# A router product of 16 rows, with the halves added on VectorE

## The chip, the cores and the metric

The kernel runs on one core of a Trainium2 chip. The metric is the device time of one execution in microseconds (us), as the median of several runs. TensorE (PE) does the matmuls and the transposes, VectorE (DVE) and ScalarE (ACT) the elementwise work and what is taken out of TensorE's banks, GpSimd (POOL) some preparation and the indirect transfers, SyncE (SP) issues the other transfers.

## The reference, cut to what matters

An attention layer (gated, in groups of 64 tokens, with a linear part over the whole sequence) is followed by a residual and a layer norm, a mixture of experts on its output, another residual and norm. The router chooses two of eight experts for each token, from eight logits a token:

```
x = _layernorm(x + attention(x, ...))       # 8 blocks of 512 tokens, 256 wide
shared = new_gelu(xf @ Wfc_s + bfc_s) @ Wproj_s + bproj_s
logits = xf @ Wr                            # Wr: 256 x 8
probs = jax.nn.softmax(logits, axis=-1)
topk_p, topk_i = jax.lax.top_k(probs, 2)
...                                         # gates from topk_p, eight experts, summed
x = _layernorm(x + shared + routed)
```

A wrong choice of an expert would be a large error, so the logits have to be as exact as the other products.

## The kernel before, in words

TensorE's products use a rounded format (`F32R`). To come near full precision each operand is split: a high part (the rounded value) and a low part (the value less its high part). A product is then three matmuls, high by low, low by high and high by high, which add up in one bank (`three`, lines 675 to 679).

The program has two parts with a barrier between them. The first, `attention`, goes over the eight blocks of 512 tokens in steps b = 0 to 10. Step b does the attention of block b, the output product and second norm of block b - 1, and transposes, splits and routes block b - 2. Steps 3 to 6 are a loop at run time (`Fori`), the others are written out. From step 8 on, the shared expert's first products are laid beside the rest. The second part, `experts`, begins with the softmax over all logits and does everything else.

Each engine has a list of its own, written by hand, and does it in order. What ties the lists together are semaphores: an instruction counts one up when it is done, another waits for a number. A wait holds all that stands behind it on the same engine. There is no planner: the order in the source is the order on the engine.

The path of the logits for block c = b - 2:

- At the end of step b TensorE multiplies the router's weights with the transposed x1 (line 844). The result, 8 experts by 512 tokens, stands in rows 0 to 7 of bank 7. The count is `lt_mm`.
- ScalarE, after the last rounding of `u`, copies it to `lgT` (line 488, recorded as line 378, `lt_ev`). `lgT` has 128 rows, of which the others are zero.
- In step b + 1 TensorE, after the value products, transposes `lgT` in four tiles of 128 tokens into bank 7 (lines 746 to 750, `lg_mm`).
- ScalarE, after the last value block, copies the 8 columns of each tile to `logits` (line 440, recorded as line 378, `lg_ev`), and goes on with the normalised x1 and the next block's xn (`normed`, line 396).
- TensorE meanwhile is in the output product (lines 755 to 765). Its four token tiles go to the halves of banks 6 and 7. The third (t = 2) writes bank 7, so it waits for `lg_ev` (line 758). After it come the keys and scores, the gate products, the key-value product, the transposes and the product of `u`.

VectorE in a step: statistics and reciprocal roots for two norms (`stats`, `rstd`), the rotary embedding and the heads (lines 562 to 571), the residual's addition (line 575), statistics of the output product straight from its banks (line 576), the norm (581, 585), the attention scores, the low parts. The list of a step then begins anew. A `link` makes VectorE wait for its own operation, where the next reads what it wrote.

Of the kernel before, what the change touches and what calls it, by code (L numbers as in the profile page):

```python
# [23 lines left out]
F32 = mybir.dt.float32  # L24
F32R = mybir.dt.float32r
# [3 lines left out]
ALU = mybir.AluOpType  # L29
# [3 lines left out]
P = 128  # L33
B, T, D = 8, 512, 256
# [6 lines left out]
NE = 8  # L41
KD = D // P
KE = E // P
KH = HID // P
TT = T // P
# [25 lines left out]
def is_int(n):  # L71
    return isinstance(n, int)
# [111 lines left out]
def attention(nc, a, shared):  # L184
    ident, ones2, logits = (shared[k] for k in ("ident", "ones2", "logits"))
# [5 lines left out]
    with ExitStack() as ctx:  # L191
# [11 lines left out]
                                                   ("wg", [P, KD, E]), ("wo", [P, KE, D])))  # L203
        wrh, wrl = pair("wr", [P, KD, NE])
        bv2 = sb("bv2", [P, E], F32R)
# [16 lines left out]
        z = sb("z", [P, TT, D])  # L222
        lgT = sb("lgT", [P, T])
        x1 = sb("x1", [P, TT, D])
        x1T = sb("x1T", [P, KD, T])
# [151 lines left out]
        def _(act):  # L377
# [35 lines left out]
            def step(b):  # L413
# [22 lines left out]
                if at(B + 2):  # L436
                    beside(7)
                if not is_int(b) or b >= 3:
                    act.wait_ge(lg_mm, b - 2)
                    copy(logits[:, bass.ds((b - 3) * TT, TT), :], bank[7][:, :].rearrange("p (t n) -> p t n", t=TT)[:, :, 0:NE]).then_inc(lg_ev, 1)  # L440
                if last:
# [44 lines left out]
                if last:  # L486
                    act.wait_ge(lt_mm, c + 1)
                    copy(lgT[0:NE, :], bank[7][0:NE, :]).then_inc(lt_ev, 1)
                if at(B):
# [12 lines left out]
        def _(dve):  # L502
# [32 lines left out]
            def beside(*chunks):  # L535

                for j in chunks:
                    dve.wait_ge(hh_rd, j + 1)
                    tt(e_hl[j % 4], e_h[j % 2], e_hh[j % 4].bitcast(F32), ALU.subtract).then_inc(hl_rd, 1)

            def step(b):
                main, ahead, o, last = stages(b)
# [18 lines left out]
                if main:  # L561
                    for s in range(2):
                        dve.wait_ge(q_ev, 4 * b + 2 * s + 2)
                        last_i = tt(qkr[:, s, :], qk[:, s, :], rope[:, s, :], ALU.mult)
                        last_i.then_inc(qkr_rd, 1)
                    dve.wait_ge(qkr_rd, 2 * b + 1)
                    stt(heads[:, 0, :], qkr[:, 0, :], vec[:, GQ:GQ + 1], offs[:, 0, :], ALU.mult, ALU.add)
                    link(stt(heads[:, 1, :], qkr[:, 0, :], vec[:, GK:GK + 1], offs[:, 1, :], ALU.mult, ALU.add))
                    dve.wait_ge(qkr_rd, 2 * b + 2)
                    stt(heads[:, 1, :], qkr[:, 1, :], vec[:, GK + 1:GK + 2], heads[:, 1, :], ALU.mult, ALU.add).then_inc(heads_rd, 1)  # L570
                    stt(heads[:, 0, :], qkr[:, 1, :], vec[:, GQ + 1:GQ + 2], heads[:, 0, :], ALU.mult, ALU.add).then_inc(heads_rd, 1)
                if o:
                    yo = [bank[6 + t // 2][:, t % 2 * D:t % 2 * D + D] for t in range(TT)]
# [84 lines left out]
            bias_rows(bpj[SHW][0:BR, :], bpj_raw[SHW][:, :])  # L658
            link(nc.vector.tensor_copy(wrh[:, :, :], wr[:, :, :]))
            tt(wrl[:, :, :], wr[:, :, :], wrh[:, :, :].bitcast(F32), ALU.subtract).then_inc(tab_rd, 1)  # L660
            step(1)
# [5 lines left out]
            link.end(B - 4)  # L667
            for b in range(B - 1, B + 2):
                step(b)

        @block.tensor
        def _(pe):
# [46 lines left out]
            def step(b):  # L719
# [113 lines left out]
                if last:  # L833
# [9 lines left out]
                    for k in range(KD):  # L843
                        last_i = three(bank[7][0:NE, :], wrh[:, k, :], wrl[:, k, :], x1h[:, k, :], x1l[:, k, :], k == 0, k == KD - 1)
                    last_i.then_inc(lt_mm, 1)
# [12 lines left out]

STEP_LINKS, BLOCK_LINKS, SMALL_LINKS = 33, 10, 6

# [756 lines left out]
```

## Time and profile before

| | us |
|---|---|
| median of 3 runs | 1000.14 |
| lowest, highest | 999.05, 1000.84 |
| the profiled execution | 1000.27 |
| its span, first to last instruction | 998.4 |
| TensorE busy | 936.1 (94%) |
| VectorE busy | 752.9 (75%) |
| ScalarE busy | 566.6 (57%) |
| attention part | to about 337 of the span |

TensorE's matmuls are pipelined: one starts before the one ahead has ended, so the distance of two starts is what a matmul costs, and its duration in a row is longer. A square bracket at the end of a row of the order of time says how long the engine was idle before it, and what ended that.

### The profile page before, as it was taken

To read this page: it belongs to the slowest core of one execution; us is meant where nothing else is said; L and a number is where in the kernel's file an instruction comes from. 1 tells how busy PE (TensorE), PEld (TensorE's weight loads), DVE (VectorE), ACT (ScalarE), POOL (GpSimd) and SP (SyncE) were. 2 spreads that over 40 slices of the span, in tenths; PEclk is the share of its full clock that TensorE was granted. 3 is DMA by queue.
4 is the path that set the end of the run, shared out by engine and by line. 5 is a ranking of instruction groups with operands and counts; after the bars stand their busy time and mean duration, and the time that the engine had idled before them with its cause. 6 is when DMAs were issued, how large, how long until landed. Compare 5 with 4: busy or idle time off the path is not lost.

```text
span 998.4 us, 17975 instructions
## 1 busy us (share of the span) xinstructions
PE 936.1 (94%) x5998; PEld 830.3 (83%) x5998; DVE 752.9 (75%) x1823; ACT 566.6 (57%) x1008; POOL 234.3 (23%) x170
## 2 busy tenths in 40 slices
PE   4979999999997988899999999999999989999995
PEld 3767788788876777799999999999999989999994
DVE  5799889888876589677777777777777879984846
ACT  5625556655645532355555555555555768874654
POOL 0050000000000000324444444444444444421000
PEclk9979999999999998999999999999999999999998
DMA  4130323231333422245555555555555678877302
GB/s 155 58 117 30 129 69 126 68 127 52 106 114 126 145 44 85 72 130 127 133 138 132 141 155 147 132 134 135 136 143 143 177 194 226 237 223 222 106 22 85
DMA packets 66869, 125.88 MB, mean 126 GB/s; under 512 B 13629, under 2 KB 52384, under 8 KB 60289
## 3 DMA queue, kind: packets, MB, share of 16 engines
q1 hardware_dynamic: 48144, 101.02, 30.4%
q0 software_dynamic: 14976, 20.54, 12.4%
q10 hardware_dynamic: 3696, 3.67, 1.1%
q8 instruction: 28, 0.46, 0.2%
q14 instruction: 25, 0.20, 0.1%
HBM read 92.40 MB, written 31.75 MB: 124 GB/s over the span
## 4 chain that ended last, share of the span: by engine, by line
PE 57%; DVE 6%; ACT 1%; DMA 1%; issue 1%; POOL 0%; DVEq 0%
PE bank L1460 28%; PE bank L1503 27%; PE bank L1488 2%; DVE s_hl L1382 1%; DVE s_acc L1256 1%; DMA s_xb<-x_rows,s_token 1%; DVE s_until_map L1258 1%; DVE s_until_map L1257 1%; DVE s_acc L1344 0%; POOL residual_sums L1080 0%; ACT s_hh L1130 0%; PE bank L1457 0%; ACT s_h L1126 0%; DVE s_until_map L1259 0%; PE bank L1523 0%
## 5 line engine op out<-in xcount | busy, mean ns | idle before, releaser
L1126 ACT ACTIVATE s_h<-bank,k_bfc 128x512 f32<-128x512 f32 (+1 forms) x248 | 154.6, 623 | 248.0 <-PE bank L1503 236.2
L1382 DVE TENSOR_TENSOR s_hl<-s_h,s_hh 128x512 fp32r<-128x512 f32 (+1 forms) x248 | 151.8, 613 | 144.0 <-ACT s_hh L1130 142.9
L1080 POOL DMA_INDIRECT residual_sums<-s_y,s_dest x78 | 132.8, 1703 | 233.0 <-DVE s_y L1330 216.6
L1071 POOL DMA_INDIRECT s_xb<-x_rows,s_token x78 | 84.8, 1087 | 382.3 <-DVE s_dest L1272 342.3
L1130 ACT ACTIVATE s_hh<-s_h 128x512 fp32r<-128x512 f32 (+1 forms) x248 | 141.4, 570 | 11.4 <-ACT s_h L1126 1.4
L1503 PE MATMUL bank<-k_uh,k_wfc1h 128*128 128x512 f32 (+1 forms) x448 | 139.6, 361 | 0.5 <-PEq L191 0.5
L1460 PE MATMUL bank<-s_wpj0l,s_hh 128*128 128x256 f32 x448 | 126.0, 281 | 1.4 <-DVE s_hl L1382 1.4
L1460 PE MATMUL bank<-s_wpj0h,s_hh 128*128 128x256 f32 x448 | 126.0, 281 | 0.0
L1460 PE MATMUL bank<-s_wpj0h,s_hl 128*128 128x256 f32 x448 | 125.8, 281 | 0.0
L1460 PE MATMUL bank<-k_wpj1l,s_hh 128*128 128x256 f32 x400 | 113.2, 283 | 0.2 <-DVE s_hl L1382 0.2
L1460 PE MATMUL bank<-k_wpj1h,s_hh 128*128 128x256 f32 x400 | 113.1, 283 | 0.0
L1460 PE MATMUL bank<-k_wpj1h,s_hl 128*128 128x256 f32 x400 | 113.0, 283 | 0.0
L1503 PEld LDWEIGHTS bank<-k_uh,k_wfc1h 128*128 128x128 f32 x448 | 82.5, 190 | 10.4 <-issue 0.6
L1460 PEld LDWEIGHTS bank<-s_wpj0l,s_hh 128*128 128x128 f32 x448 | 84.5, 189 | 5.5 <-DVE s_hl L1382 1.6
L1460 PEld LDWEIGHTS bank<-s_wpj0h,s_hl 128*128 128x128 f32 x448 | 85.5, 191 | 3.4
L1460 PEld LDWEIGHTS bank<-s_wpj0h,s_hh 128*128 128x128 f32 x448 | 84.4, 188 | 0.0
L1503 PE MATMUL bank<-k_xTl,s_wfc0h 128*128 128x512 f32 (+1 forms) x224 | 83.7, 374 | 0.6 <-issue 0.6
L1503 PE MATMUL bank<-k_xTh,s_wfc0l 128*128 128x512 f32 (+1 forms) x224 | 81.3, 363 | 0.0
L1503 PE MATMUL bank<-k_xTh,s_wfc0h 128*128 128x512 f32 (+1 forms) x224 | 80.8, 361 | 0.0
L1503 PE MATMUL bank<-k_uh,k_wfc1l 128*128 128x512 f32 (+1 forms) x224 | 79.8, 356 | 0.0
L1460 PEld LDWEIGHTS bank<-k_wpj1l,s_hh 128*128 128x128 f32 x400 | 75.8, 189 | 3.9 <-DVE s_hl L1382 0.6
L1460 PEld LDWEIGHTS bank<-k_wpj1h,s_hl 128*128 128x128 f32 x400 | 75.6, 189 | 3.3
(297 smaller groups left out, 2159.2 us busy)
## 6 DMA issues: line engine op xcount, KB each, us to landing
k_wstage<-wall SPq DMA_DIRECT2D x50, 1024.0 KB, 5.6
s_x_in<-x SPq DMA_DIRECT2D x8, 512.0 KB, 4.2
s_x_res<-x SPq DMA_DIRECT2D x8, 512.0 KB, 4.7
x_rows<-s_x SPq DMA_DIRECT2D x8, 512.0 KB, 3.5
residual_sums<-s_x SPq DMA_DIRECT2D x8, 512.0 KB, 4.2
x_parts<-s_x1h SPq DMA_DIRECT2D x8, 512.0 KB, 2.6
x_parts<-s_x1l SPq DMA_DIRECT2D x8, 512.0 KB, 3.7
k_uh<-x_parts SPq DMA_DIRECT2D x8, 512.0 KB, 4.9
```

The lines of the kernel that those rows point to most:

```text
L1071: pool.indirect_dma_start(xb[i][:, t, :], None, X1D, bass.IndirectOffsetOnAxis(token[:, at:at + 1].bitcast(U32), 0), bounds_check=N - 1).t ...
L1080: pool.indirect_dma_start(RES, bass.IndirectOffsetOnAxis(dest[:, at:at + 1].bitcast(U32), 0), y[:, t, :], None, bounds_check=N + S - 1, co ...
L1126: nc.scalar.activation(h[j % 2][:, cols], b[:, cols], ACT.Gelu_apprx_tanh, bias=bfc[w][:, j:j + 1]).then_inc(h_ev, 1)
L1130: nc.scalar.activation(hh[j % RING][:, cols], h[j % 2][:, cols], ACT.Copy).then_inc(hh_rd, 1)
L1256: tt(pick[:, at, :], row_of(IOTA, P), each(flat(slot_p[:, :, :]), P), ALU.is_equal)
L1257: link(tt(row, row_of(IOTA + P, COLS), each(flat(slot_c[:, :, :]), COLS), ALU.is_equal))
L1258: link(tt(signed, row, each(cst[:, CODE:CODE + 2 * NT][:, at], COLS), ALU.mult))
L1382: tt(hl[j % RING][:, cols], h[j % 2][:, cols], hh[j % RING][:, cols].bitcast(F32), ALU.subtract).then_inc(hl_rd, 1)
L1460: last = mm(o, hs[p][:, cols], wpj[w][ws][:, j, :], start=r is not None and j == 0 and p == 0 and t % 2 == 0, stop=j == KH - 1 and p == 2, ...
L1488: last = nc.tensor.transpose(b[:, t * P:(t + 1) * P], xb[1 - i][:, t, j * P:(j + 1) * P], ident[:, :])
L1503: last = mm(b[:, cols], wfc[w][ws][:, c, rows_], xs[i][:, c, cols], start=c == 0 and p == 0, stop=c == KD - 1 and p == 2)
```

## The change

The router's high and low weights stand side by side in one tile `wr_parts` of 16 columns. For each of the two halves of the contraction the product is now two matmuls: all 16 columns with the high part of x1 (high by high in rows 0 to 7, low by high in rows 8 to 15), and the 8 high columns with its low part, added to rows 0 to 7. The copy to `lgT` and the transposes carry 16 rows. The two halves are added after the transposes: `router_logits` on VectorE copies the lower half out of the bank to `lg_lo`, and adds it to the upper half into `logits`. ScalarE's copy at that place is gone. `router_logits` stands in VectorE's list between the heads and the residual's addition, and VectorE has a step more at the end.

```diff
-        wrh, wrl = pair("wr", [P, KD, NE])
+        wr_parts = sb("wr_parts", [P, KD, 2 * NE], F32R)
+        lg_lo = sb("lg_lo", [P, TT, NE])
@@ ScalarE, step
-                if not is_int(b) or b >= 3:
-                    act.wait_ge(lg_mm, b - 2)
-                    copy(logits[:, bass.ds((b - 3) * TT, TT), :], bank[7][:, :].rearrange("p (t n) -> p t n", t=TT)[:, :, 0:NE]).then_inc(lg_ev, 1)
...
-                    copy(lgT[0:NE, :], bank[7][0:NE, :]).then_inc(lt_ev, 1)
+                    copy(lgT[0:2 * NE, :], bank[7][0:2 * NE, :]).then_inc(lt_ev, 1)
@@ VectorE
+            def router_logits(c):
+
+                dve.wait_ge(lg_mm, c + 1)
+                by_tile = bank[7][:, :].rearrange("p (t n) -> p t n", t=TT)
+                link(nc.vector.tensor_copy(lg_lo[:, :, :], by_tile[:, :, NE:2 * NE]))
+                tt(logits[:, bass.ds(c * TT, TT), :], by_tile[:, :, 0:NE], lg_lo[:, :, :], ALU.add).then_inc(lg_ev, 1)
...
                     stt(heads[:, 0, :], qkr[:, 1, :], vec[:, GQ + 1:GQ + 2], heads[:, 0, :], ALU.mult, ALU.add).then_inc(heads_rd, 1)
+                if not is_int(b) or b >= 3:
+                    router_logits(b - 3)
                 if o:
...
-            link(nc.vector.tensor_copy(wrh[:, :, :], wr[:, :, :]))
-            tt(wrl[:, :, :], wr[:, :, :], wrh[:, :, :].bitcast(F32), ALU.subtract).then_inc(tab_rd, 1)
+            link(nc.vector.tensor_copy(wr_parts[:, :, 0:NE], wr[:, :, :]))
+            tt(wr_parts[:, :, NE:], wr[:, :, :], wr_parts[:, :, 0:NE].bitcast(F32), ALU.subtract).then_inc(tab_rd, 1)
...
-            for b in range(B - 1, B + 2):
+            for b in range(B - 1, B + 3):
                 step(b)
@@ TensorE, step
                     for k in range(KD):
-                        last_i = three(bank[7][0:NE, :], wrh[:, k, :], wrl[:, k, :], x1h[:, k, :], x1l[:, k, :], k == 0, k == KD - 1)
+                        mm(bank[7][0:2 * NE, :], wr_parts[:, k, :], x1h[:, k, :], start=k == 0, stop=False)
+                        last_i = mm(bank[7][0:NE, :], wr_parts[:, k, 0:NE], x1l[:, k, :], start=False, stop=k == KD - 1)
```

On VectorE, in the loop (steps 3 to 6), this is what stands from the last two operations of the heads on, before the change:

```order
L570 SCALAR_TENSOR_TENSOR s_heads<-s_qkr,s_vec,s_heads 128x512 [waits qk_roped]
L571 SCALAR_TENSOR_TENSOR s_heads<-s_qkr,s_vec,s_heads 128x512
L574 REGISTER_ALU
L575 TENSOR_TENSOR s_x_res<-s_x_res,s_ln 128x1024 [waits residual_loaded]
L576 ISA
L519 BN_STATS s_st<-bank 128x6 [waits o_product]
```

And after it, where the heads' lines are 575 and 576 and the residual's addition is line 582:

```order
L575 SCALAR_TENSOR_TENSOR s_heads<-s_qkr,s_vec,s_heads 128x512 [waits qk_roped]
L576 SCALAR_TENSOR_TENSOR s_heads<-s_qkr,s_vec,s_heads 128x512
L541 REGISTER_ALU
L543 COPY s_lg_lo<-bank 128x32 [waits logits_transposed]
L102 REGISTER_ALU
L544 ISA [waits vector_own]
L544 TENSOR_TENSOR k_logits<-bank,s_lg_lo 128x32
L581 REGISTER_ALU
L582 TENSOR_TENSOR s_x_res<-s_x_res,s_ln 128x1024 [waits residual_loaded]
L583 ISA
L517 BN_STATS s_st<-bank 128x6 [waits o_product]
```

The copy and the addition have come between the heads and the residual's addition, with the wait for the copy between them.

On ScalarE in the same steps, from the last value block on, before:

```order
L435 ACTIVATE s_v<-bank 128x512 [waits v_product]
L439 REGISTER_ALU
L378 ISA [waits logits_transposed]
L378 ACTIVATE k_logits<-bank 128x32
L442 REGISTER_ALU
L90 REGISTER_ALU [waits scales_ready]
L396 ACTIVATE s_x<-s_z,s_shift,s_rs 128x256 [waits x1_stored]
```

And after:

```order
L436 ACTIVATE s_v<-bank 128x512 [waits v_product]
L440 REGISTER_ALU
L90 ISA [waits scales_ready]
L397 ACTIVATE s_x<-s_z,s_shift,s_rs 128x256 [waits x1_stored]
```

ScalarE no longer waits for the transposes; the normalised x1 follows the value blocks directly. On TensorE the third tile of the output product keeps its wait (`logits_ready`), which is now counted by VectorE's addition.

## Rows read from the trace of the kernel before

**Rows 1.** Busy time by stretch: engines, clock, DMA share, GB/s

```profile
120.00:280.00 160.00, 160.00 (x919) 131.22 (x918) 134.89 (x395) 97.20 (x170) 0.00 (x0) 1.00 0.28 92
280.00:337.00 57.00, 49.08 (x301) 41.26 (x300) 32.75 (x105) 27.79 (x49) 0.00 (x0) 0.94 0.42 141
```

**Rows 2.** Order of time (start, duration, engine, line, operation), TensorE, end of step 2

```profile
120.29 0.40 PE L679 MATMUL bank<-s_x1h,s_wrh 128*8 128x512 f32 x1
...
121.21 0.39 PE L677 MATMUL bank<-k_xTl,s_wqkh 128*128 128x512 f32 x1
```

**Rows 3.** Order of time, step 3: third output tile and VectorE

```profile
132.67 0.28 PE L761 MATMUL bank<-s_bo,k_ones 128*128 128x256 f32 x1
...
133.35 1.22 DVE L575 TENSOR_TENSOR s_x_res<-s_x_res,s_ln 128x1024 f32<-128x1024 f32 x1
...
135.95 0.76 DVE L519 BATCH_NORM_STATS2 s_st<-bank 128x6 f32<-128x256 f32 x2 [0.71 <-PE bank L679]
```

**Rows 4.** Order of time, VectorE, end of step 3

```profile
149.18 0.69 DVE L528 TENSOR_TENSOR k_xTl<-s_xT,k_xTh 128x512 fp32r<-128x512 f32 x1 [1.17 <-ACT k_xTh L378]
```

**Rows 5.** Order of time, the same two places in step 6

```profile
234.42 0.28 PE L761 MATMUL bank<-s_bo,k_ones 128*128 128x256 f32 x1
...
235.04 1.22 DVE L575 TENSOR_TENSOR s_x_res<-s_x_res,s_ln 128x1024 f32<-128x1024 f32 x1
```

**Rows 6.** VectorE: line 1189 by itself, then order of time at three places

```profile
L1189 DVE TENSOR_TENSOR s_gates<-s_cnt x2: 189/192/195, 351.2 to 351.3; 128x32 f32<-128x32 f32 x2
...
410.05 0.23 DVE L1267 COPY s_found<-bank 128x78 f32<-128x78 f32 x1
410.31 0.24 DVE L1268 SCALAR_TENSOR_TENSOR s_code<-s_found,bank 128x78 f32<-128x78 f32 x1
...
410.97 0.23 DVE L1271 TENSOR_TENSOR s_code<-s_empty,s_cst 128x78 f32<-128x78 f32 x1
...
164.99 0.74 DVE L568 SCALAR_TENSOR_TENSOR s_heads<-s_qkr,s_vec,s_offs 128x512 f32<-128x512 f32 x1
165.85 0.75 DVE L570 SCALAR_TENSOR_TENSOR s_heads<-s_qkr,s_vec,s_heads 128x512 f32<-128x512 f32 x1
```

**Rows 7.** Order of time: TensorE waits for VectorE at 341 us

```profile
341.07 0.69 DVE L1382 TENSOR_TENSOR s_hl<-s_h,s_hh 128x512 fp32r<-128x512 f32 x1 [1.29 <-ACT s_hh L1130]
...
341.81 0.39 PE L1457 MATMUL bank<-k_bpj,k_ones 128*128 128x256 f32 x1 [0.70 <-DVE s_hl L1382]
342.04 0.29 PE L1460 MATMUL bank<-k_wpj1l,s_hh 128*128 128x256 f32 x1
```

**Rows 8.** Order of time, the two places in step 7

```profile
267.11 1.22 DVE L575 TENSOR_TENSOR s_x_res<-s_x_res,s_ln 128x1024 f32<-128x1024 f32 x1
...
268.33 0.28 PE L761 MATMUL bank<-s_bo,k_ones 128*128 128x256 f32 x1
```

**Rows 9.** Order of time, step 8, TensorE and VectorE

```profile
291.50 0.66 PE L749 MATMUL bank<-k_ident,s_lgT 128*128 128x128 f32 x4 [0.68 <-ACT s_lgT L378]
...
295.07 0.28 PE L761 MATMUL bank<-s_bo,k_ones 128*128 128x256 f32 x1
...
296.10 0.16 DVE L523 SCALAR_TENSOR_TENSOR s_shift<-s_mean,s_rs 128x4 f32<-128x4 f32 x1
...
298.79 1.41 DVE L519 BATCH_NORM_STATS2 s_st<-bank 128x6 f32<-128x256 f32 x4
...
307.33 0.58 PE L707 MATMUL bank<-k_bpj,k_ones 128*128 128x256 f32 x1 [3.99 <-DVE s_wvh L539]
```

**Rows 10.** Order of time, step 9, ScalarE and TensorE

```profile
321.20 0.20 ACT L378 ACTIVATE k_logits<-bank 128x32 f32<-128x32 f32 x1 [0.49 <-PE bank L749]
...
323.40 1.22 PE L684 MATMUL bank<-k_ident,s_x 128*128 128x128 f32 x8 [2.25 <-ACT s_x L396]
```

**Rows 11.** Busy time by stretch, in steps 1 and 9

```profile
75.00:80.00 5.00, 3.74 (x10) 1.58 (x9) 4.77 (x14) 0.69 (x1) 0.00 (x0) 1.00 0.00 0
324.00:328.00 4.00, 4.00 (x18) 3.42 (x17) 1.29 (x2) 2.94 (x6) 0.00 (x0) 0.57 0.96 330
```

More of the change, by code:

```diff
@@ L855, in _ @@
             steps(pe, step, end=B + 3)
-STEP_LINKS, BLOCK_LINKS, SMALL_LINKS = 33, 10, 6
+STEP_LINKS, BLOCK_LINKS, SMALL_LINKS = 34, 10, 6
 def experts(nc, a, out, shared):
```

## The prediction

> **What bounds the kernel now.** I read the busy time by stretch first. In the attention part (up to 337 us) TensorE is busy without a break from 120 to 280 us, at full granted clock, while VectorE and ScalarE are not full; only in the last 57 us of that part has TensorE holes [rows 1]. So in the steps of the loop a microsecond taken from TensorE's order, or put into it, is a microsecond of the kernel, unless the part's own order of waits says otherwise. The rest of the kernel (661 us) is not touched, and starts behind a barrier that TensorE reaches last. All that matters lies in the steps b = 2 to 9 and the short step 10.
>
> The next view is the order of time in single steps, and there one distance decides. The output product of a step has four token tiles; the third writes bank 7, in which the router's transposed logits stand, so it waits on the count that says that the logits are taken out. In step 3 it starts at 132.67 us [rows 3]. VectorE at that time is still at the rotary heads, and starts the next thing, the residual's addition of line 575, only at 133.35. The same distance stands in all four steps that wait so (3 to 6): 0.68 us in the first, 0.62 in the last [rows 3, 5]. This order costs nothing today, because ScalarE takes the logits.
>
> **The change, part by part.**
>
> *The product.* Two products of 512 columns for each half of the contraction take the place of three. The router's products follow one another like the others: from the third at 120.29 to the first of the next group at 121.21 are four starts, 0.23 us each [rows 2], and that although each has only 8 rows of output. Sixteen rows instead of 8 should change nothing in that. Two products less are 0.46 us of TensorE in each of eight steps, 3.7 us in all, if each counts.
>
> *The logits move from ScalarE to VectorE*, and stand in VectorE's order behind the heads: a copy of the lower half out of the bank, a wait for the copy, an addition that releases TensorE. Nothing like them stands there in the trace, so I bound them. An operation on 128x32 takes 0.19 us [rows 6]. Behind a linked operation the next started 0.03 us after its end in straight code (410.05 + 0.23 to 410.31) and 0.12 us after it in the loop, where register instructions stand between (164.99 + 0.74 to 165.85) [rows 6]. From VectorE's end to TensorE's start are 0.05 us (341.07 + 0.69 to 341.81), and the product behind such a wait then needs 0.23 us until the next starts, where 0.12 is usual for 256 columns: 0.11 us to get going again [rows 7]. I take 0.19 + 0.12 + 0.19 + 0.05 = 0.55 us from the old start of line 575 to TensorE's start, and 0.11 for the restart. The low end is the straight-code gap and no restart, 0.46; the high end has 0.23 for each operation (the 78-wide ones), a gap of 0.12 ahead of the copy too, and the restart: 0.86.
>
> At 78 elements a copy out of a bank took 0.23 us and an addition out of SBUF (410.97) 0.23 us as well, so the bank is no dearer a source here [rows 6]. The Trainium skill (VectorE: DVE Perf Modes, the section on the errata of trn2) gives a source in PSUM 62 cycles more than one in SBUF, an estimate of 0.065 us each at its clock. By that rule the two operations would cost 0.13 us more in a step than the 0.19 of an operation out of SBUF, and the sum would be 0.5 us higher.
>
> *Steps 3 to 6: a new wait.* Does VectorE come earlier because TensorE does? No: its work in a step begins with line 528, for which it waits 1.17 us on ScalarE's rounding of the transposed input [rows 4], which hangs on TensorE's work of the step before, ahead of the router's product; from there to line 575 I see no idle time on it worth naming. So VectorE's time is fixed against TensorE's past, and TensorE, 0.46 us earlier, only waits longer. Its third tile starts at (line 575's old start) + 0.55: that is 0.65 (mean of 0.68 and 0.62) + 0.55 = 1.20 us later than today, plus 0.11. The 0.46 us saved are already swallowed in this. Four steps by 1.31 are **+5.2 us**, with 4 x (0.65 + 0.46) = 4.4 and 4 x (0.65 + 0.86) = 6.0 as ends. The idle time that TensorE shows is 1.20 + 0.46 = 1.7 us each time. What stands behind it in its order (second half of the output product, keys, gate) is as late. VectorE is not made later still: its addition and first statistics end about 0.5 us later, and it has to wait for the second half of the product anyway (0.71 us today [rows 3], about 1.4 then).
>
> *Step 7.* It is the last with attention, and has no statistics of a further input, so VectorE is early: line 575 starts at 267.11 and the third tile at 268.33 [rows 8]. The pair ends at about 267.6, TensorE comes at 267.9. No wait; the product of step 6 is worth its **-0.46**. With a pair of 0.86 us it would be 0.1 late, so this term is safe.
>
> *Step 8.* The saving of the product of step 7 is worth nothing: TensorE waits 0.68 us today for ScalarE's copy of it [rows 9], and ScalarE is held by VectorE there; if the copy did follow, it would be -0.46. The logits now come behind a whole normalisation on VectorE. Its last operation starts at 296.10; plus about 0.1 to the copy and 0.46 that is 296.7, where the third tile starts at 295.07 today [rows 9]. TensorE stops 1.6 us and ends the product at 295.07 + 1.6 + 0.1 + 26 x 0.12 = 299.9. Most is covered: VectorE reads the second half at 298.79 + 2 x 0.35 = 299.5 today [rows 9], and would then at 299.9 + 0.2 = 300.1 (the 0.2 as in step 3: 132.67 + 3.1 against 135.95 [rows 3]). VectorE's chain from there is what TensorE waits 3.99 us for at 307.33 [rows 9]. So **+0.54**, from 0.3 to 0.8. Its cover is the wait for the residual's transfer ahead of line 575; without it the pair would add its own 0.4.
>
> *Steps 8 and 9: the products*, in stretches where TensorE is busy up to the next wait: **-0.46** and **-0.46**.
>
> *Step 9, ScalarE.* Today it waits 0.49 us for TensorE's transposes and takes the logits in 0.20 us ahead of the normalised x1, for which TensorE then waits 2.25 us [rows 10]. Both go; as neighbours on an engine overlap by some 0.09 us, I count **-0.6**. What is late next is the same normalisation, then held by ScalarE's rounding ahead of it. In step 10 VectorE's new pair lies beside TensorE's last products.
>
> **Sum:** 5.2 - 0.46 + 0.54 - 0.46 - 0.46 - 0.6 = +3.8 us. On the profiled execution (span 998.4, time 1000.27) this gives 1004.0; the median of the runs is 0.13 lower, so 1003.9 us. The ends of the terms give +2.3 (4.4 in the loop, 0.3 in step 8, step 7's product worth 0.46 too) to +4.9 (6.0, 0.8): 1002.4 to 1005.0.
>
> **Rivals.**
>
> *The saving counts in full* (7%). If VectorE's pair were done when TensorE comes, all would be gain: 8 x 0.46 + 0.6 = 4.3 us, **995.8 us**, faster. The place is the third tile of steps 3 to 6; it decides whether the addition is finished by 132.67 - 0.46 = 132.2 in step 3. For it: VectorE has idle time elsewhere in the step (busy 135 of 160 us [rows 1]). Against it: it would have to come 1.7 us earlier, and the idle time lies ahead of line 528.
>
> *It nearly balances* (8%): something in VectorE's order moves up by 1 us, say because ScalarE is rid of its wait, and each stop shrinks to 0.3 us net. Then 4 x 0.3, less the 1.4 of the other terms (3 x 0.46 + 0.6 - 0.54), gives about **1000 us**, no difference. Against it: ScalarE's earlier start does not feed the heads.
>
> *The clock stays up in step 9* (14%). After the idle 2.25 us the granted clock was 0.57 on the mean of 4 us, so near its level of 1.2 GHz for most of them, a loss of 4 x 0.43 = 1.7 us; in step 1, in a stretch of 5 us with 1.26 us idle (3.74 busy), it stayed at 1.00, 2.4 GHz [rows 10, 11]. The idle time shrinks to 1.65, between the two. If that suffices: **1002.2 us**, at the edge of what can be told.
>
> *The clock falls in the new waits* (9%). They are 1.6 to 1.7 us, again between those two rows, each with TensorE busy for over 30 us until the next. If it fell after each (five) by the same 1.7 us: 1003.9 + 8.5 = **1012 us**; after that in step 8 alone, where another wait is close ahead, 1005.6. The Trainium skill (TensorE: Matmul & The Clock Gate, Part 1) says that an array left idle goes back to half clock; the rows show both outcomes, and by the rule alone I could not choose.
>
> **How the numbers follow.** The forecast has 62%, and 1003.9 is its time; its own range is 1002.4 to 1005.0. The range for 8 in 10 takes in most of the case with the clock up below and the single fallen clock above: 1001.5 to 1006.5. What a measurement of this kernel can tell from no change is 0.2%, 2.0 us. Faster: 0.07. Same: 0.08 and half of the 14%, 0.15. Slower: 0.78.
>
> **What would show it.** In the changed profile TensorE would have, at the third output tile of steps 3 to 6, four waits of about 1.7 us on VectorE's addition, and one of 1.6 in step 8; none in step 7. The copy would start where the residual's addition now does and be followed by the addition 0.3 us later. The distance from step to step, 33.9 us now, would be about 35.2 in the loop. ScalarE's lower copy would be gone and TensorE's wait in step 9 at 1.65 us. I am wrong if these waits are missing or below 0.6 us, if the clock falls behind them, or if the part after the barrier changes by over a microsecond.

## The result, and the profile after

| | before | after |
|---|---|---|
| median of 6 runs each, us | 999.96 | 1002.59 |
| lowest, highest | 999.05, 1000.84 | 1001.39, 1004.44 |
| the profiled execution, us | 1000.27 | 1002.44 |
| its span | 998.4 | 1000.6 |

The ratio is 1.0033, interval 1.0021 to 1.0045: slower by 2.6 us measured, 2.2 us between the two profiled executions. The prediction said 1003.9 us, in a range of 1001.5 to 1006.5.

The time can be laid out by landmarks on TensorE, which both traces have. They are the first tile of the output product in each step, the first shared-expert product behind step 8 (line 707, then 714), the transposes of x1 in step 9 (684, then 691), and the first matmul behind the barrier (1503, then 1511). Each number is the distance of two starts in the order of time.

| stretch | before | after | difference |
|---|---|---|---|
| start to step 2's output product | 95.73 | 95.43 | -0.30 |
| step 2 to step 3 | 33.77 | 33.31 | -0.46 |
| step 3 to step 7, four steps | 135.67 | 141.01 | +5.34 |
| step 7 to step 8 | 26.74 | 26.73 | 0 |
| step 8 to the shared expert's product | 15.42 | 16.06 | +0.64 |
| from there to the transposes of x1 | 16.07 | 15.00 | -1.07 |
| from there to the barrier's far side | 13.35 | 11.32 | -2.03 |
| the rest | 661.65 | 661.74 | +0.09 |

The differences add up to the 2.2 us between the spans. The mean step of the loop, in what follows, is the third stretch over four: 33.92 us before and 35.25 after. Now the rows, in the order of the program. By stretch, of the profile after (start:end, length, then PE, PEld, DVE, ACT and POOL busy, granted clock, DMA share, GB/s):

```profile
120.00:280.00 160.00, 153.93 (x891) 127.41 (x890) 131.67 (x395) 93.91 (x162) 0.00 (x0) 1.00 0.28 91
280.00:339.00 59.00, 50.94 (x312) 42.35 (x312) 38.12 (x121) 29.11 (x50) 0.00 (x0) 0.97 0.40 137
```

TensorE, without a break from 120 to 280 us in [rows 1], now has 6.1 us of holes there, at the same clock. The waits of TensorE from 94 us to the end of the attention part say what they are (in total, times, longest):

```profile
PE bank L768 <- DVE k_logits L544: 7.5, 5, 1.6
PE bank L714 <- DVE s_wvh L537: 2.9, 1, 2.9
PE bank L691 <- ACT s_x L397: 1.6, 1, 1.6
PE bank L756 <- ACT s_lgT L379: 1.1, 1, 1.1
```

The first row has no counterpart before: five waits, 7.5 us, on VectorE's addition, four of them in this stretch and one in step 8. The page's first part, of the profile after:

```profile
PE 931.3 (93%) x5982; PEld 827.1 (83%) x5982; DVE 756.0 (76%) x1839; ACT 565.1 (56%) x1000; POOL 234.8 (23%) x170
```

TensorE's busy time fell from 936.1 to 931.3 us, with 16 matmuls less, and the span rose. Busy time says here only that the saving was made, not that it arrived. The router's product, in the order of time at the end of step 2, answers to [rows 2]:

```profile
119.45 0.48 PE L851 MATMUL bank<-s_x1h,s_wr_parts 128*16 128x512 f32 x1
119.76 0.40 PE L852 MATMUL bank<-s_x1l,s_wr_parts 128*8 128x512 f32 x1
120.00 0.40 PE L851 MATMUL bank<-s_x1h,s_wr_parts 128*16 128x512 f32 x1
120.23 0.40 PE L852 MATMUL bank<-s_x1l,s_wr_parts 128*8 128x512 f32 x1
120.46 0.40 PE L684 MATMUL bank<-k_xTl,s_wqkh 128*128 128x512 f32 x1
```

From the second start on they follow at 0.23 to 0.24 us, whether with 16 rows or with 8. Step 3, VectorE and TensorE, answers to [rows 3]:

```profile
132.41 0.74 DVE L576 SCALAR_TENSOR_TENSOR s_heads<-s_qkr,s_vec,s_heads 128x512 f32<-128x512 f32 x1
133.07 0.18 DVE L543 COPY s_lg_lo<-bank 128x32 f32<-128x32 f32 x1
133.42 0.19 DVE L544 TENSOR_TENSOR k_logits<-bank,s_lg_lo 128x32 f32 x1 [0.17 <-DVE s_lg_lo L543]
133.54 1.23 DVE L582 TENSOR_TENSOR s_x_res<-s_x_res,s_ln 128x1024 f32<-128x1024 f32 x1
133.66 0.39 PE L768 MATMUL bank<-s_bo,k_ones 128*128 128x256 f32 x1 [1.59 <-DVE k_logits L544]
...
137.05 0.76 DVE L517 BATCH_NORM_STATS2 s_st<-bank 128x6 f32<-128x256 f32 x2 [1.62 <-PE bank L686]
```

The copy starts as soon as the last operation of the heads lets it, the addition 0.35 us later, TensorE another 0.24 later. VectorE then waits 1.62 us for the second half of the product, 0.71 before: it pays nothing for the pair, TensorE pays all. Step 8, after, answers to [rows 9]:

```profile
300.69 0.16 DVE L521 SCALAR_TENSOR_TENSOR s_shift<-s_mean,s_rs 128x4 f32<-128x4 f32 x1
300.99 0.19 DVE L544 TENSOR_TENSOR k_logits<-bank,s_lg_lo 128x32 f32<-128x32 f32 x1
301.24 0.39 PE L768 MATMUL bank<-s_bo,k_ones 128*128 128x256 f32 x1 [1.43 <-DVE k_logits L544]
...
312.54 0.39 PE L714 MATMUL bank<-k_bpj,k_ones 128*128 128x256 f32 x1 [2.92 <-DVE s_wvh L537]
```

TensorE stops 1.43 us for the addition, and then has 2.92 us to wait where it had 3.99. The 1.07 us between them are what that later wait absorbs. Step 9, after, answers to [rows 10]:

```profile
325.43 2.06 ACT L397 ACTIVATE s_x<-s_z,s_shift,s_rs 128x256 f32<-128x256 f32 x4
327.54 1.09 PE L691 MATMUL bank<-k_ident,s_x 128*128 128x128 f32 x8 [1.57 <-ACT s_x L397]
```

And the six microseconds behind it (TensorE alone: length, busy, granted clock, DMA share, GB/s):

```profile
327.54:333.54 6.00, 6.00 (x36) 1.00 0.85 315
```

Here is the one thing that the forecast's sum did not have. The wait is 1.57 us instead of 2.25, and TensorE's clock is at 2.4 GHz behind it, where [rows 11] show 0.57.

### The profile page after: what moved, and what is told of

Read it like the earlier page. It is cut to its first block, busy times and chain, and to the rows that moved or that the text cites. A ratio compares the mean times of both kernels' runs of the same rounds, so it can differ in the third digit from the quotient of the medians.

```text
span 1000.6 us, 17955 instructions
## 1 busy us (share of the span) xinstructions
PE 931.3 (93%) x5982; PEld 827.1 (83%) x5982; DVE 756.0 (76%) x1839; ACT 565.1 (56%) x1000; POOL 234.8 (23%) x170
## 4 chain that ended last, share of the span: by engine, by line
PE 57%; DVE 6%; issue 1%; ACT 1%; DMA 1%; POOL 0%; DVEq 0%
PE bank L1468 28%; PE bank L1511 27%; PE bank L1496 2%; DVE s_hl L1390 1%; DVE s_acc L1264 1%; DMA s_xb<-x_rows,s_token 1%; DVE s_until_map L1266 1%; DVE s_until_map L1265 1%; DVE s_acc L1352 0%; POOL residual_sums L1088 0%; ACT s_hh L1138 0%; ACT s_h L1134 0%; PE bank L1465 0%; DVE s_until_map L1267 0%; PE bank L1531 0%
```

## The experiments

Three theories stood against each other. The first is that of the prediction: TensorE waits because the pair stands behind the heads in VectorE's order. The second: VectorE has more work, wherever it stands. The third: the product of 16 rows and its transposes are dearer. Each run has the ratio to the kernel before, measured on the same chip in the same session.

**e1_early.** The pair goes ahead of the heads in steps 3 to 7, and ahead of a normalisation in step 8. Nothing is left out.

```diff
@@ VectorE, step
+                if at(B):
+                    router_logits(b - 3)
                 if ahead:
...
                         last_i.then_inc(qkr_rd, 1)
+                    if not is_int(b) or b >= 3:
+                        router_logits(b - 3)
                     dve.wait_ge(qkr_rd, 2 * b + 1)
...
-                if not is_int(b) or b >= 3:
+                if is_int(b) and b > B:
                     router_logits(b - 3)
```

> The changed kernel with the same copy and addition on VectorE, but earlier in its order: in the steps with attention behind the rotary products and ahead of the heads, in step 8 behind the statistics of z. Theory 1 (TensorE waits for the place in VectorE's order): the pair is done at about 130.8 in step 3 and TensorE comes at 132.2, so all five waits at the third output tile are gone and eight products less count, 7 x 0.46 (that of step 7 is swallowed by ScalarE) and 0.6 of ScalarE: 3.8 us less than before, 996.2, ratio 0.996; 1.7 less still where the clock stays up in step 9. Theory 2 (VectorE is nearly full, and 0.4 us more work a step on it is what costs): the same work at another place stays at about 1002.6, ratio 1.003. Theory 3 (two products do not save, as 16 rows are dearer): about 999.5 to 1000.

Measured: 994.08 us against 999.38, ratio 0.9945 (0.9931 to 0.9958). The expectation holds, in its version with the clock up in step 9: behind that wait the granted clock is 1.00. In the order of time of step 3, VectorE's pair and TensorE's third tile:

```profile
130.46 0.18 DVE L543 COPY s_lg_lo<-bank 128x32 f32<-128x32 f32 x1
...
130.81 0.19 DVE L544 TENSOR_TENSOR k_logits<-bank,s_lg_lo 128x32 f32 x1 [0.17 <-DVE s_lg_lo L543]
...
132.19 0.28 PE L772 MATMUL bank<-s_bo,k_ones 128*128 128x256 f32 x1
```

The addition is done 1.2 us before TensorE comes, and there is no bracket on the third tile. VectorE does the same work, in the same loop, so the second theory falls. A step of the loop takes 33.47 us, 0.45 less than before: the saving counts in full once nothing waits for it.

**e2_product_only.** Two products instead of three, but ScalarE takes the upper half of the logits at its old place, and nothing is done on VectorE. The lower half (low weights by high x1) is left out of the logits.

```diff
@@ against the kernel after, ScalarE, step
+                if not is_int(b) or b >= 3:
+                    act.wait_ge(lg_mm, b - 2)
+                    copy(logits[:, bass.ds((b - 3) * TT, TT), :], bank[7][:, :].rearrange("p (t n) -> p t n", t=TT)[:, :, 0:NE]).then_inc(lg_ev, 1)
@@ VectorE, step
-                if not is_int(b) or b >= 3:
-                    router_logits(b - 3)
```

> The kernel before with the two products of 16 and 8 rows, and ScalarE taking the upper half of the logits at its old place; the lower half is left out of the sum. Theory 1: seven of eight products less count by 0.46 us each, -3.2 us, 996.8, ratio 0.9968; TensorE never waits at the third tile. Theory 3 (16 rows are dearer): no gain, 1000. Theory 2 says nothing against -3.2.

Measured: 996.02, ratio 0.9964 (0.9951 to 0.9977). A step of the loop is 33.47 us. The third theory falls: 16 rows cost what 8 cost.

**e3_move_only and e11_move_again.** The kernel before with its three products, but the copy of the logits moved to VectorE, behind the heads. Nothing is left out. The second label is the same kernel in another session.

```diff
@@ against the kernel before, ScalarE, step
-                if not is_int(b) or b >= 3:
-                    act.wait_ge(lg_mm, b - 2)
-                    copy(logits[...], bank[7][...][:, :, 0:NE]).then_inc(lg_ev, 1)
@@ VectorE, step, behind the heads
+                if not is_int(b) or b >= 3:
+                    dve.wait_ge(lg_mm, b - 2)
+                    nc.vector.tensor_copy(logits[...], bank[7][...][:, :, 0:NE]).then_inc(lg_ev, 1)
...
-            for b in range(B - 1, B + 2):
+            for b in range(B - 1, B + 3):
```

> The kernel before with three products as they are, and only the copy of the logits moved from ScalarE to VectorE behind the heads (one operation, no addition). Theory 1: TensorE waits at the third tile of steps 3 to 6 for 0.65 + 0.19 + 0.05 = 0.9 us and pays 0.11 to get going, +4.0 us; none in step 7; +0.4 in step 8; -0.6 in step 9 by ScalarE: +3.8 us, 1003.8, ratio 1.0038, or 1.7 less where the clock stays up in step 9. Theory 2 (work on VectorE): 0.2 us a step on it, at most +1 us, and less the 0.6: about 1000.5.

> The move of the logits' copy alone once more, as its time (1.0005) was below the 1.0038 (1.0021 with the clock up in step 9) expected, while its profile showed the waits and the step of 34.87 us. Theory 1: from the first output product to the barrier again 2.0 us more than before, and a ratio of 1.001 to 1.003 when the time behind the barrier is 661 to 662 as in the others. If the time behind the barrier is again 659.3, this kernel meets the rest with a luckier clock, and the ratio stays at 1.0005.

Measured: 1000.52 against 999.38, ratio 1.0005 (0.9991 to 1.0018); the second time 1001.87 against 999.59, ratio 1.0029 (1.0014 to 1.0043). In step 3 of e3_move_only:

```profile
134.07 0.18 DVE L571 COPY k_logits<-bank 128x32 f32 x1
...
134.31 0.39 PE L761 MATMUL bank<-s_bo,k_ones 128*128 128x256 f32 x1 [0.74 <-DVE k_logits L571]
```

One copy at that place, alone and with no saving ahead of it, stops TensorE for 0.74 us (0.9 were expected). The step is 34.87 us, 0.95 more than before. The place is enough to produce the wait. The expected ratio, 1.0038 or 1.0021, was missed in the first session and met in the second. In the trace of e3_move_only the loop costs 3.8 us more than before, step 9 gives back 2.2 (below), and the part behind the barrier, where nothing was changed, is 2.3 us shorter (659.38 against 661.68). In that of e11_move_again the way from step 2's output product to the barrier's far side is only 0.55 us longer than before, where 2.0 were expected: the clock stayed up in step 8 too. The mean granted clock on record for each run goes with the times: of the first session's twelve runs of this kernel the four at 0.979 took 1001.7 to 1002.3 us, the eight at 0.983 to 0.986 took 997.3 to 1000.8; in the second the two at 0.984 took 998.7 and 999.0, the six at 0.979 to 0.982 took 1001.5 to 1003.5. How often a session meets the higher clock moves its median, and the sign of this kernel's time is less sure than its trace.

**e4_pe_adds.** TensorE adds the halves: in place of the transposes, four products of `lgT` (16 rows) with two identities of 8 stacked on each other; ScalarE takes the logits at its old place. Nothing is left out.

```diff
@@ against the kernel after, TensorE, step
-                        last_i = tr(bank[7][:, t * P:(t + 1) * P], lgT[:, t * P:(t + 1) * P], ident[:, :])
+                        last_i = mm(bank[7][:, t * P:t * P + NE], lgT[0:2 * NE, t * P:(t + 1) * P], pile[0:2 * NE, :], start=True, stop=True)
@@ VectorE, ahead of the steps
+            tt(pile[0:2 * NE, :], ident[0:2 * NE, 0:NE], ident[0:2 * NE, NE:2 * NE], ALU.add)
```

> Two products as in the change, and the halves added by TensorE: in place of the transposes of four tiles against the identity, four products of the 16 rows with a 16 by 8 matrix of two identities on top of each other give the sum of the halves; ScalarE takes it at its old place. Theory 1: as with the product alone, 7 x 0.46 less, 996.8; the transposes cost 0.36 us a step today, and with 8 columns in place of 128 could cost 0.1 less, so down to 996. If four small products cost more than the transposes (a product of unrounded operands stands as two instructions in the trace of line 776), up to 998.

Measured: 1000.23, ratio 1.001 (0.9998 to 1.0022): the expectation missed. Step 3 shows why:

```profile
128.28 1.05 PE L751 MATMUL bank<-s_pile,s_lgT 16*128 16x8 f32 x8
129.26 0.38 PE L763 MATMUL bank<-s_bo,k_ones 128*128 128x256 f32 x1
```

The four small products take 0.98 us until the next starts (and stand as eight instructions), where the four transposes took 0.36. That gives away the 0.46 saved and 0.16 more; the step, 34.14 us, is 0.22 above before, and the other 0.06 are not accounted for. Fewer rows and columns were not cheaper, though a product and a transpose may differ in more than their size, which was not tried.

**e5_after_again.** The kernel after, unchanged, in another session.

> The changed kernel once more, beside the others. Theory 1: ratio to before 1.002 to 1.0045 again; in its profile the third output tile of steps 3 to 6 starts 1.2 to 1.4 us later than TensorE's order would have it, and the step is 35.2 us long, as in the first profile (35.24, 35.23, 35.21), since both hang on the program's order. The clock in step 9 (1.00 in the first profile of the change, 0.57 before) may be either: it is a matter of the moment, and if so the time outside the loop differs by 1 to 2 us between two profiles of the same kernel.

Measured: 1002.75 against 999.0, ratio 1.0038 (1.0024 to 1.0052), a step of 35.22 us. The slowdown holds.

**e6_copy_twice.** The kernel after with the copy of the lower half made twice, one after the other, each with its wait.

```diff
                 link(nc.vector.tensor_copy(lg_lo[:, :, :], by_tile[:, :, NE:2 * NE]))
+                link(nc.vector.tensor_copy(lg_lo[:, :, :], by_tile[:, :, NE:2 * NE]))
```

> The changed kernel with the copy of the lower half made twice, each with its wait, so that the pair is a triple. Theory 1 (TensorE waits for the end of the last): the copy to addition distance measured in the loop is 0.34 us, so each of the four waits grows by 0.34 and the step to 35.56 us; +1.4 us in the loop, +0.2 in step 8 after its cover, none in step 7 (0.36 us of room there, 0.22 used): +1.6 us against the changed kernel, ratio about 1.005. Theory 2 (VectorE's load): 0.34 us a step on VectorE in all eight steps, that it makes up in its idle time; the step stays at 35.2.

Measured: 1004.3, ratio 1.0057 (1.0039 to 1.0076). In step 3:

```profile
133.40 0.18 DVE L543 COPY s_lg_lo<-bank 128x32 f32<-128x32 f32 x1
133.62 0.19 DVE L544 COPY s_lg_lo<-bank 128x32 f32<-128x32 f32 x1
133.98 0.19 DVE L545 TENSOR_TENSOR k_logits<-bank,s_lg_lo 128x32 f32 x1 [0.17 <-DVE s_lg_lo L544]
134.22 0.38 PE L769 MATMUL bank<-s_bo,k_ones 128*128 128x256 f32 x1 [1.81 <-DVE k_logits L545]
```

The second copy starts 0.22 us after the first, and TensorE's wait grows from 1.59 to 1.81 us. The step is 35.45, 0.20 more than in the first trace of the kernel after and 0.23 more than in e5_after_again: what VectorE has at this place, TensorE pays one for one. The expected 0.34 took the distance from copy to addition for that of any linked pair. It is not: from copy to copy are 0.22 us, from copy to addition 0.36. In straight code (step 7 of the kernel after, below) copy to addition are 0.22 too. In the loop the addition's output has an address that is computed there; that this is the cause was not tried.

**e7_early_loop.** The pair early in steps 3 to 7, late in step 8 as in the kernel after. That is e1_early without its first two added lines, and with `b > B - 1` at the late place.

> As the early version in steps 3 to 7, but in step 8 the pair stands behind the normalisation, as in the change. Theory 1: the step is 33.5 us long in the loop (33.92 less 0.46), no wait there; in step 8 one wait of about 1.4 us at the third tile, of which 0.5 to 0.65 us reach the end: 0.6 us more than the early version, ratio 0.995.

Measured: 995.57 against 999.0, ratio 0.9968 (0.9957 to 0.9979), a little above the 0.995 expected. The loop is as expected, 33.45 us a step and no wait. To the shared expert's product step 8 takes 16.03 us, 0.63 more than in e1_early (15.40). That is the price of the late place in step 8. It does not stay: the stretch behind it takes 15.00 instead of 15.94. What differs there is the clock. Of TensorE in e1_early, then in e7_early_loop, that product with the wait ahead of it (order of time), and the six microseconds behind it (length, busy, granted clock, DMA share, GB/s):

```profile
305.01 0.58 PE L718 MATMUL bank<-k_bpj,k_ones 128*128 128x256 f32 x1 [3.96 <-DVE s_wvh L537]
```

```profile
305.02:311.02 6.00, 6.00 (x23) 0.54 0.53 137
```

```profile
305.02 0.39 PE L716 MATMUL bank<-k_bpj,k_ones 128*128 128x256 f32 x1 [2.90 <-DVE s_wvh L537]
```

```profile
305.02:311.02 6.00, 6.00 (x28) 0.72 0.61 163
```

Twenty-three matmuls start in one stretch and twenty-eight in the other, and e12_early_again repeats the lower clock (0.54 behind a wait of 4.09 us, 15.93 us). But the length of the wait does not settle it at this place. The same two views of e11_move_again:

```profile
311.19 0.39 PE L707 MATMUL bank<-k_bpj,k_ones 128*128 128x256 f32 x1 [2.90 <-DVE s_wvh L536]
```

```profile
311.20:317.20 6.00, 6.00 (x39) 1.00 0.60 163
```

The same wait as in e7_early_loop, and a full clock behind it. e4_pe_adds waits 3.37 us there and has 1.00 too; the kernel before waits 3.99 and has 0.73.

**e8_step9.** The kernel before, with one change: in step 9 ScalarE takes the logits behind the normalised x1.

```diff
@@ against the kernel before, ScalarE, step
-                if not is_int(b) or b >= 3:
+                def take():
                     act.wait_ge(lg_mm, b - 2)
                     copy(logits[...], bank[7][...][:, :, 0:NE]).then_inc(lg_ev, 1)
+                if (not is_int(b) or b >= 3) and not at(B + 1):
+                    take()
                 if last:
                     act.wait_ge(scale_rd, b + 2)
                     need(act, x1_st, 32 * (b - 2))
                     normed(x1, z, TT, x1_rd)
+                if at(B + 1):
+                    take()
```

> The kernel before, with ScalarE in step 9 taking the logits behind the normalised x1 instead of ahead of it; nothing else. Theory 1: TensorE's wait for x1 falls from 2.25 to about 1.6 us, -0.6 us, ratio 0.9994. If the length of that wait decides whether the clock falls (0.57 after it before), it now stays up and 1.6 us more are gained: ratio 0.998. If the clock falls by chance of the moment, the profile may show either.

Measured: 997.86 against 999.0, ratio 0.9986 (0.9972 to 1.0), between the two values expected and at the edge of what can be told. The trace tells more. TensorE's transposes in step 9 and the six microseconds behind them, in e8_step9:

```profile
323.49 1.09 PE L688 MATMUL bank<-k_ident,s_x 128*128 128x128 f32 x8 [1.57 <-ACT s_x L396]
```

```profile
323.50:329.50 6.00, 6.00 (x36) 1.00 0.88 315
```

The same in e10_before_again:

```profile
323.98 1.24 PE L684 MATMUL bank<-k_ident,s_x 128*128 128x128 f32 x8 [2.25 <-ACT s_x L396]
```

```profile
324.00:330.00 6.00, 6.00 (x30) 0.72 0.87 313
```

And in e2_product_only:

```profile
320.19 0.98 PE L684 MATMUL bank<-k_ident,s_x 128*128 128x128 f32 x7 [2.24 <-ACT s_x L396]
```

```profile
320.20:326.20 6.00, 6.00 (x36) 1.00 0.88 315
```

From the transposes to the barrier e8_step9 takes 11.76 us, before 13.35, with the same three products: the raised clock is worth 1.6 us. Over all kernels: ten traces have a wait of 1.6 us here, and all ten have 1.00 behind it. Four have 2.25 us (before, e10_before_again, e4_pe_adds, e2_product_only); three of them have 0.72 behind it, and e2_product_only has 1.00. So the clock stayed up behind the shorter wait every time, and the longer one did not always cost it. What decides behind the longer one is not shown.

**e9_mid.** The pair one operation earlier than in the kernel after: between the last two of the heads.

```diff
                     stt(heads[:, 1, :], ..., heads[:, 1, :], ALU.mult, ALU.add).then_inc(heads_rd, 1)
+                    if not is_int(b) or b >= 3:
+                        router_logits(b - 3)
                     stt(heads[:, 0, :], ..., heads[:, 0, :], ALU.mult, ALU.add).then_inc(heads_rd, 1)
-                if not is_int(b) or b >= 3:
+                if is_int(b) and b >= B:
                     router_logits(b - 3)
```

> The changed kernel with the pair one operation earlier in VectorE's order in the steps with attention: ahead of the last operation of the heads instead of behind it; in steps 8 to 10 as in the change. Theory 1: the heads' operations start 0.66 us apart, so each of the four waits is 0.66 us shorter (0.85 to 0.95 instead of 1.5 to 1.6) and the step in the loop 34.57 instead of 35.23 us: 2.6 us less than the changed kernel, ratio about 1.001. Theory 2 (VectorE's load): no difference to the changed kernel, 1.0035.

Measured: 1000.49 against 999.59, ratio 1.0013 (1.0003 to 1.0023). In step 3:

```profile
132.85 0.19 DVE L544 TENSOR_TENSOR k_logits<-bank,s_lg_lo 128x32 f32 x1 [0.17 <-DVE s_lg_lo L543]
133.09 0.39 PE L770 MATMUL bank<-s_bo,k_ones 128*128 128x256 f32 x1 [0.93 <-DVE k_logits L544]
```

Moving past an operation of 0.66 us (from its start to the next) takes 0.66 off TensorE's wait (1.59 to 0.93), and 0.65 to 0.68 off the step, 34.57 us. Together with e1_early it shows that the wait follows the place, and by how much.

**e10_before_again.** The kernel before, unchanged, as a run of its own.

> The kernel before, against itself: ratio 1.000 within 0.15%. Its second profile shows whether the fallen clock in step 9 is there again (wait 2.25 us, mean clock of the 6 us behind it 0.72), and how much the time behind the barrier (661.7 us in the first profile) differs between two profiles of the same program: by the first profiles of the other kernels, 659.3 to 662.6, up to 3 us by the clock alone.

Measured: 999.0, ratio 0.9996 (0.9985 to 1.0007). Its step is 33.91 us (33.92 in the first trace). The four kernels that were traced twice repeat their step to 0.01 to 0.03 us. The fallen clock in step 9 is there again.

**e12_early_again.** The kernel of e1_early in another session.

> The early version once more, beside the kernel before: ratio 0.994 to 0.997 (first 0.9945; 0.62% faster by 3.8 us of products and ScalarE and 1.6 of the clock in step 9 is 0.9946, without the clock 0.9962). In its profile no wait at the third output tile, and the clock at 1.00 behind the 1.6 us wait in step 9.

Measured: 996.77 against 999.59, ratio 0.9967 (0.9956 to 0.9978). It is the faster order in both sessions, by 0.55% and by 0.33%, and in both faster than the kernel after. In the traces the attention part is alike (236.57 and 236.62 us from step 2's output product to the barrier's far side), but the part behind the barrier takes 662.33 and 664.61: the difference of the two traces lies where nothing was changed. That of the sessions goes with the granted clock: three of the first five runs stood at 0.981 (993.7 to 994.1 us) and two at 0.977 (996.2 and 996.5), while nine of the second twelve stood at 0.976 to 0.979 (995.6 to 998.8) and three at 0.980 to 0.982 (993.8 to 995.8).

The mean step of the loop sums the experiments up; between the rows nothing else was changed in the loop than the second column says:

| kernel | products; where the logits are taken | step, us |
|---|---|---|
| before, e10_before_again | 3; ScalarE | 33.92, 33.91 |
| e2_product_only | 2; ScalarE | 33.47 |
| e1_early, e7_early_loop, e12_early_again | 2; VectorE, ahead of the heads | 33.47, 33.45, 33.45 |
| e4_pe_adds | 2, four dearer ones; ScalarE | 34.14 |
| e9_mid | 2; VectorE, within the heads | 34.57 |
| e3_move_only, e11_move_again | 3; VectorE, one copy behind the heads | 34.87, 34.89 |
| after, e5_after_again | 2; VectorE, the pair behind the heads | 35.25, 35.22 |
| e6_copy_twice | 2; VectorE, the pair and a copy more | 35.45 |

## Why the prediction was right

*The product, 0.46 us.* Shown: e2_product_only and e1_early each take 0.45 off the step, and the first product gives 33.77 to 33.31 in the kernel after.

*Steps 3 to 6, +5.2 us, and -0.46 for step 7.* Together that is 4.8 up to step 7's output product. Measured is -0.46 (the product of step 2, which the prediction counted as swallowed in the first wait) + 5.34 = 4.88. The step was to be 35.2 us and is 35.25. From the copy's start to TensorE's are 0.59 us, where 0.55 was counted. The idle time was to be 1.7 us and is 1.5 (four waits, 7.5 less the 1.43 of step 8): the bracket counts from the modelled end of the matmul ahead, 0.28 us after its start, and not from the 0.12 at which the next would have come. Those 0.16 and the 0.11 of the restart make up what the step loses above its idle time: 33.47 to 35.25 are 1.78, against 1.52. The reason given was that VectorE is not made earlier by the saved 0.46. It is borne out: from e3_move_only to the kernel after, the step grows by 0.38, which is the addition behind the copy (0.35), and of the saved product nothing is seen.

*Step 7, no wait.* Shown in the order of time after; VectorE is through, and the third tile has no bracket:

```profile
272.15 0.19 DVE L543 COPY s_lg_lo<-bank 128x32 f32<-128x32 f32 x1
272.37 0.19 DVE L544 TENSOR_TENSOR k_logits<-bank,s_lg_lo 128x32 f32<-128x32 f32 x1
...
272.92 0.28 PE L768 MATMUL bank<-s_bo,k_ones 128*128 128x256 f32 x1
```

*Step 8, +0.54.* It is +0.64, with a stop of 1.43 us where 1.6 was forecast; with the 0.16 that the bracket leaves out, the two agree. The prediction's own figures (299.9 + 0.2 against 299.5) give 0.6 and not 0.54, and the upper ends of its terms add up to 4.8 and not 4.9; neither matters. The product of step 7 was worth nothing, as forecast: the wait for `lgT` grew from 0.68 to 1.14 us, by the 0.46.

```profile
296.07 0.66 PE L756 MATMUL bank<-k_ident,s_lgT 128*128 128x128 f32 x4 [1.14 <-ACT s_lgT L379]
```

*Steps 8 and 9: product and ScalarE, -0.46 and -0.6.* The stretch is -1.07, and TensorE's wait for ScalarE in step 9 is 1.57 where 1.65 was forecast.

*The bank as a source.* The copy out of the bank takes 0.18 us in the loop and the addition, half of it from the bank, 0.19, as an operation out of SBUF did [rows 6]. The dearer price that the Trainium skill (VectorE: DVE Perf Modes, the section on the errata of trn2) gives a source in PSUM does not show in these durations.

*What was missed.* Step 9's clock. The prediction had it as a rival with 14%, worth 1.7 us; it came true and is worth 1.6. It is the whole distance between the forecast sum of +3.8 and the traces' +2.2: the other terms and the part behind the barrier came out 0.3 us higher together, and the first 96 us 0.3 lower, for no reason that I can name. That the forecast had the sign and nearly the size of the change is the work of the loop's term. The rival that the clock falls behind the new waits did not come about: the granted clock is 1.00 from 120 to 280 us, with four waits of 1.5 to 1.6 us, and 1.00 again from 300 to 312 us, behind the one in step 8. The two rivals in which the pair is done in time, or nearly, fall with the rows of step 3; e1_early and e12_early_again show that the first was to be had at another place in the same list.

*What stays open.* The measured difference, 2.6 and 3.75 us in two sessions, is above the 2.2 of the traces. The measured times of the same kernel also differ between sessions (0.24% in e3_move_only against e11_move_again, 0.22% in e1_early against e12_early_again); these differences go with the granted clock of the runs, as told above, but what sets that clock behind the barrier is not shown. Why the kernel after measures more than its traces differ by is open: its runs in e5_after_again stood at 0.979 to 0.982, no lower than the kernel before beside them (sixteen of 24 at 0.979). The forecast of 1003.9 is 1.3 us above the median, with a step's mechanism that is confirmed and a clock term that is not in it; that the two nearly meet is partly this open remainder.

## What to carry to other kernels

A saving on the full engine is lost when the work that pays for it goes behind another engine's queue: before moving an operation, compare the start of the instruction that waits for it with the time at which the new engine gets there, and look up its order for a place (here one operation up still left a wait of 0.93 us in step 3, and four operations up left none). The same two operations cost 1.8 us a step at one place (35.25 against 33.47) and nothing 2.9 us earlier in the step (the copy 1.44 us behind the step's first output tile instead of 4.33). What an edit does to waits far behind it, the clock among them, has to be added in: here the clock gave back 1.6 us.

## What the runs showed of the hardware

- Four products of 16 rows by 8 columns in plain f32 took 0.98 us, in eight instructions; four transposes of 128x128 took 0.36. These tiny products were not cheap ones.
- Of two linked operations on 128x32 on VectorE, the second started 0.22 us after the first in straight code, and in the loop 0.22 where it was a copy and 0.35 to 0.36 where it was the addition.
- In step 9, behind an idle 1.6 us, TensorE's clock was at 2.4 GHz in all ten traces; behind 2.25 us it was lower (0.72 over 6 us) in three of four. In step 8, behind 2.9 us, it was lower (0.72) in six of seven traces and full in the seventh, behind 3.37 us full in one trace, and behind 3.96 to 4.33 us lower in all six (0.54 to 0.73).
- Runs of one kernel differed by up to 5 us, and where they did, the mean granted clock differed too: in e3_move_only they took 1001.7 to 1002.3 us at 0.979, and 997.3 to 1000.8 us at 0.983 to 0.986.
